# A cross-attention block on one core: values from a second copy of the context, their last rows as a pair, and one head scaled by VectorE

## What is computed

```
h = layernorm(x, gamma, beta)                       # x: 8 x 256 x 256
Q = h @ Wq;  K = context @ Wk;  V = context @ Wv    # context: 8 x 256 x 192; 1024 columns each
attn = softmax(Q K^T per head) * 64 ** -0.5
out = x + (attn V) @ Wo + bo
```

## Time and profile before

| | |
|---|---|
| median of 3 runs | 335.07 us (335.03 to 335.29) |
| the profiled execution | 335.13 us |
| its span, first to last instruction | 333.3 us |
| TensorE busy | 323.3 us, 97% |
| VectorE busy | 234.6 us, 70% |
| ScalarE busy | 254.8 us, 76% |
| GpSimd busy | 178.3 us, 53% |
| granted TensorE clock | 1.0, the 2.4 GHz level |

### The profile page before, as it was taken

How to read it: one execution, slowest core, us unless ns; L and a number is a source line. 1 busy time by engine, 2 the same in 40 slices (tenths; PEclk the granted TensorE clock), 3 DMA queues, 4 the chain that set the end, 5 groups by cost and what they waited for, 6 DMA issues and landing times.

```text
span 333.3 us, 9654 instructions
## 1 busy us (share of the span) xinstructions
PE 323.3 (97%) x3773; PEld 284.3 (85%) x3773; DVE 234.6 (70%) x523; ACT 254.8 (76%) x799; POOL 178.3 (53%) x332
## 2 busy tenths in 40 slices
PE   5999999999999999999999999999999999999986
PEld 4868788899888899888889988889988888998864
DVE  5888667766778677676776677776677867556754
ACT  4899897777778766888667868777777876676772
POOL 4596778437473367543673456722757336344430
PEclk9999999999999999999999999999999999999999
DMA  6960010020000200020000200002000100000000
GB/s 181 266 185 3 1 41 18 2 89 2 0 2 31 60 3 0 2 89 2 3 4 0 89 2 2 0 3 89 2 2 1 33 3 3 2 0 33 2 3 31
DMA packets 10764, 10.70 MB, mean 32 GB/s; under 512 B 960, under 2 KB 10176, under 8 KB 10720
## 3 DMA queue, kind: packets, MB, share of 16 engines
q1 hardware_dynamic: 10192, 9.64, 9.6%
q10 hardware_dynamic: 416, 0.33, 0.3%
q0 software_dynamic: 112, 0.13, 0.1%
HBM read 8.00 MB, written 2.10 MB: 30 GB/s over the span
## 4 chain that ended last, share of the span: by engine, by line
PE 86%; ACT 6%; DVE 4%; POOL 2%; DMA 1%; issue 1%; DVEq 0%; ACTq 0%
PE mix_ps L823 16%; PE o_ps L914 12%; PE ring_ps L794 12%; PE ring_ps L889 12%; PE ring_ps L968 11%; PE ring_ps L944 10%; PE ring_ps L847 9%; ACT prob L457 3%; DMA x_in<-in_x_dram 1%; PE ring_ps L867 1%; POOL prob L369 1%; PE mix_ps L760 1%; PE mix_ps L768 1%; ACT qk_hi L467 1%; DVE prob_t L737 1%
## 5 line engine op out<-in xcount | busy, mean ns | idle before, releaser
L369 POOL TENSOR_SCALAR prob<-prob,inv 128x256 f32<-128x256 f32 x256 | 120.4, 486 | 129.2 <-DVE inv L654 129.1
L457 ACT ACTIVATE prob<-ring_ps,neg_max 128x256 f32<-128x256 f32 x256 | 119.3, 481 | 21.7 <-DVE neg_max L647 21.6
L647 DVE TENSOR_REDUCE neg_max<-ring_ps 128x2 f32<-128x512 f32 x128 | 81.4, 679 | 0.8 <-PE ring_ps L794 0.8
L737 DVE COPY prob_t<-ring_ps 128x512 f32<-128x512 f32 x64 | 41.4, 686 | 37.0 <-PE ring_ps L944 37.0
L823 PE MATMUL mix_ps<-prob_t,v_sb 128*64 128x256 f32 x504 | 61.5, 385 | 0.2 <-DVE prob_t L737 0.2
L660 DVE TENSOR_TENSOR qk_lo<-ring_ps,qk_hi 128x512 fp32r<-128x512 f32 x64 | 44.2, 690 | 17.7 <-ACT qk_hi L467 17.7
L457 ACT ACTIVATION_READ_ACCUMULATOR prob<-ring_ps,neg_max 128x1 f32 x256 | 54.4, 212 | 0.0
L823 PEld LDWEIGHTS mix_ps<-prob_t,v_sb 128*64 128x64 f32 x504 | 33.4, 136 | 18.1 <-issue 0.3
L527 ACT ACTIVATE v_sb<-ring_ps 128x256 f32<-128x256 f32 x58 | 19.2, 383 | 30.1 <-PE ring_ps L968 29.6
L467 ACT ACTIVATE qk_hi<-ring_ps 128x512 fp32r<-128x512 f32 x64 | 39.6, 619 | 1.2 <-PE ring_ps L889 1.2
L944 PE MATMUL ring_ps<-ident,prob 64*128 64x64 f32 x1024 | 39.3, 226 | 0.3 <-POOL prob L369 0.3
(11 more groups left out here) (110 smaller groups left out, 638.2 us busy)
## 6 DMA issues: line engine op xcount, KB each, us to landing
x_in<-in_x_dram SPq DMA_DIRECT2D x8, 256.0 KB, 2.9
out_dram<-y_sb SPq DMA_DIRECT2D x7, 256.0 KB, 2.2
c_in<-in_ctx_dram SPq DMA_DIRECT2D x7, 192.0 KB, 2.8
w_raw<-in_L_xattn_Wq_dram SPq DMA_DIRECT2D x8, 128.0 KB, 3.1
w_raw<-in_L_xattn_Wo_dram SPq DMA_DIRECT2D x4, 256.0 KB, 4.0
w_raw<-in_L_xattn_Wk_dram SPq DMA_DIRECT2D x4, 128.0 KB, 3.7
w_raw<-in_L_xattn_Wk_dram SPq DMA_DIRECT2D x8, 64.0 KB, 3.5
w_raw<-in_L_xattn_Wv_dram SPq DMA_DIRECT2D x2, 256.0 KB, 4.7
```

Source lines behind the costliest of these rows:

```text
L369: last = nc.gpsimd.tensor_scalar(prob[:, e, r, :], prob[:, e, r, :], inv[:, e, r:r + 1], SCALE, ALU.mult, ALU.mult)
L457: last = nc.scalar.activation(prob[:, e, r, :], score_bank(u, e)[:, r * ROWS:(r + 1) * ROWS], ACT.Exp, bias=neg_max[:, e, r:r + 1], accum_ ...
L647: nc.vector.tensor_reduce(neg_max[:, e, :], score_bank(u, e)[:, :].rearrange("p (r j) -> p r j", r=RT), AX, ALU.max, negate=True).then_inc ...
L737: nc.vector.tensor_copy(turned_half(e), score_bank(u, e)[:, :] .rearrange("p (k i) -> p k i", i=HALF))\
```

## The change

It does five things.

- A second copy of the turned context, `c_val`, in a place of its own; GpSimd makes it with three copies per sequence (`context_for_values`), for the first sequence ahead of step 0, for the others at the end of the steps with u mod 4 = 0 (for the second in step 2). `values` reads its weights from `c_val` and waits for `c_val_ready`. The tiles behind move by 64 bytes (`wv_hi`, `wv_lo`) and by 6656 bytes (`v_sb` and all after it).
- From n = 3 on `values` makes four 128-row matmuls for each of its two banks and then, behind both, the last product as a pair of 64-row matmuls, one for each bank, from `c_rest` and the upper half of `c_val`.
- The fourth head is scaled by VectorE (`last_head`) instead of GpSimd; `turn` waits for three heads of GpSimd's and, in its second half, for VectorE's.
- From step 2 on (before: in step 2 alone) ScalarE copies `qk_hi` of the second pair ahead of the exp of head 3, and VectorE's `last_head` stands behind `qk_lo` of the second pair.
- The statistics of x are spread over their step instead of standing at its end, and those of the second sequence go to the end of step 0; its `x_norm` is made by GpSimd in step 1 instead of VectorE.

TensorE, in a step u with u mod 4 = 2: the two banks of `values` and the transposes `turn`, before, and then with the change.

The diff, without the declarations of semaphores; each piece begins with a line of "...":

```diff
...
         sb("shift4", [P, 4 * SHIFT])
         qk_lo = sb("qk_lo", [P, BATCH, 2, ROWS + SHIFT], fp32r)
-        sb("shift2", [P, 3 * SHIFT])
+        sb("shift2", [P, 4 * SHIFT])
         wv_hi = sb("wv_hi", [P, O0 - V0, INNER], fp32r)
         wv_lo = sb("wv_lo", [P, O0 - V0, INNER], fp32r)
         sb("shift3", [P, SHIFT])
+        c_val = sb("c_val", [P, 2, CT, ROWS], fp32r)
+        sb("shift5", [P, 7 * SHIFT])
         v_sb = sb("v_sb", [P, 2, RT, GROUP * P])
...
                 last.then_inc(x_norm_ready, 1)
 
+            def context_for_values(b):
+
+                if b >= 2:
+                    pool.wait_ge(v_made, PER_SEQ * (b - 1))
+                pool.wait_ge(c_lo_ready, b + 1)
+                for k in range(CT):
+                    last = nc.gpsimd.tensor_copy(c_val[:, b % 2, k, :], c_t[:, b % 2, k, :])
+                last.then_inc(c_val_ready, 1)
+
             def bias(b):
...
                 weight_lo(n)
             pool.dma_start(bo_b[:, :], b_o.partition_broadcast(P)).then_inc(bo_in, 16)
+            context_for_values(0)
 
...
                 if b is not None:
                     deviation(b)
-                    if b >= 2:
-                        norm(b)
+                    norm(b)
                 if u == PER_SEQ:
                     weight_lo(23)
                 if 0 <= u < STEPS:
-                    for e in range(HEADS):
+
+                    for e in range(HEADS - 1):
                         pool.wait_ge(inv_ready, HEADS * u + e + 1)
                         for r in range(RT):
                             last = nc.gpsimd.tensor_scalar(prob[:, e, r, :], prob[:, e, r, :],
                                                            inv[:, e, r:r + 1], SCALE,
                                                            ALU.mult, ALU.mult)
-                        last.then_inc(scaled, 1)
+                        last.then_inc(scaled_pool, 1)
                         if e == 1 and u == 2:
...
                 if b is not None:
                     hidden_lo(b)
+                b = 1 if u == 2 else of_seq(u, TURN_C, 2)
+                if b is not None:
+                    context_for_values(b)
+                b = of_seq(u, SPLIT_H, 1)
                 if u == 2:
...
                     weight_hi(20)
                     weight_hi(21)
+                if u >= 2:
                     keys_hi(1)
                 probabilities(3)
-                if u != 2:
+                if u < 2:
                     keys_hi(1)
...
                     .then_inc(w_lo_ready, 1)
 
-            def statistics(b):
+            def rows_statistics(b, r):
                 k = b % 2
                 dve.wait_ge(x_loaded[k], 16 * (b // 2 + 1))
-                for r in range(RT):
-                    last = nc.vector.bn_stats(bn[:, r, :], x_in[:, k, r, :])
-                last.then_inc(stats_done, 1)
-                dve.wait_ge(stats_done, b + 1)
+                nc.vector.bn_stats(bn[:, r, :], x_in[:, k, r, :]).then_inc(stats_done, 1)
+
+            def variance(b):
+                dve.wait_ge(stats_done, RT * (b + 1))
                 nc.vector.memset(var_eps[:, :], 0.0)
                 for r in range(RT):
                     last = nc.vector.bn_aggr(mean_var[:, r, :], bn[:, r, :])
                 last.then_inc(aggr_done, 1)
+
+            def deviation_base(b):
                 dve.wait_ge(aggr_done, b + 1)
                 nc.vector.tensor_scalar(var_eps[:, :], mean_var[:, :, 1], EPS, None, ALU.add)\
                     .then_inc(var_ready, 1)
+
+            def statistics(b):
+                for r in range(RT):
+                    rows_statistics(b, r)
+                variance(b)
+                deviation_base(b)
 
...
                         nc.vector.reciprocal(inv[:, e, :], sums[:, e, :]).then_inc(inv_ready, 1)
 
+                def last_head():
+
+                    inverse(HEADS - 1)
+                    if 0 <= u < STEPS:
+                        dve.wait_ge(inv_ready, HEADS * u + HEADS)
+                        for r in range(RT):
+                            last = nc.vector.tensor_scalar(prob[:, HEADS - 1, r, :],
+                                                           prob[:, HEADS - 1, r, :],
+                                                           inv[:, HEADS - 1, r:r + 1], SCALE,
+                                                           ALU.mult, ALU.mult)
+                        last.then_inc(scaled_vector, 1)
+
                 def keys_lo(a):
...
                 maximum(3)
                 inverse(1)
+
+                measured = of_seq(u, STATS, 2)
+                if measured is not None:
+                    rows_statistics(measured, 0)
                 b = of_seq(u, PUT)
...
                 if u == -1:
                     weight_lo(4)
+                if measured is not None:
+                    rows_statistics(measured, 1)
                 keys_lo(0)
+                if measured is not None:
+                    variance(measured)
                 if u == -1:
                     weight_lo(5)
-                if u != 2:
-                    inverse(3)
+                if u < 2:
+                    last_head()
                 b = of_seq(u, SPLIT_H, 1)
                 if b is not None:
...
-                if u == 0:
-                    statistics(1)
-                if u == 1:
-                    norm(1)
                 if u == 2:
                     weight_lo(20)
                     weight_lo(21)
                 keys_lo(1)
-                if u == 2:
-                    inverse(3)
+                if measured is not None:
+                    deviation_base(measured)
+                if u >= 2:
+                    last_head()
                 b = of_seq(u, TURN_C, 2)
                 if b is not None:
                     context_lo(b, context_bank(b))
-                b = of_seq(u, STATS, 2)
-                if b is not None:
-                    statistics(b)
                 if 0 <= u < STEPS:
...
                             .then_inc(prob_t_ready[1], 1)
                     if u == 0:
+                        statistics(1)
                         weight_lo(13)
...
 
                 for a in range(BATCH):
-                    pe.wait_ge(scaled, HEADS * u + 2 * a + 2)
+                    pe.wait_ge(scaled_pool, (HEADS - 1) * u + 2 + a)
+                    if a == BATCH - 1:
+                        pe.wait_ge(scaled_vector, u + 1)
                     for k, (h, j, r) in enumerate(itertools.product(range(2), range(RT), range(RT))):
...
 
 
+
                 g, j = divmod(n, RT)
                 b, half = divmod(g, 2)
                 rows = slice(j * P, (j + 1) * P)
                 if j == 0 and g in FOR_V:
                     high_ready(pe, FOR_V[g])
+                pe.wait_ge(c_val_ready, b + 1)
                 passes = context_products(wv_hi, wv_lo)
                 first = half * PIECE
-                for a, ps in enumerate(((mix_ps, o_ps, mix_ps)[n],) if n <= RT else qk_banks(n)):
-                    columns = PIECE if n <= RT else V_HALF
-                    if n > RT:
-
-                        pe.wait_ge(qk_lo_ready, BATCH * n + a + 1)
+                if n <= RT:
                     for m, (w, i, k) in enumerate(passes):
+                        if m == CT and j == 0:
+                            low_ready(pe, FOR_V[g])
+                        last = nc.tensor.matmul((mix_ps, o_ps, mix_ps)[n][:, :], c_val[:, b % 2, k, rows],
+                                                w[:, i, first:first + PIECE],
+                                                start=m == 0, stop=m == len(passes) - 1,
+                                                skip_group_check=True)
+                    last.then_inc(v_made, 1)
+                    return
+                for a, ps in enumerate(qk_banks(n)):
+
+                    pe.wait_ge(qk_lo_ready, BATCH * n + a + 1)
+                    for m, (w, i, k) in enumerate(passes[:-1]):
                         if m == CT and j == 0 and g in FOR_V:
                             low_ready(pe, FOR_V[g])
-                        last = nc.tensor.matmul(ps[:, 0:columns], c_t[:, b % 2, k, rows],
-                                                w[:, i, first:first + columns],
-                                                start=m == 0, stop=m == len(passes) - 1,
-                                                skip_group_check=True)
-                    first += columns
+                        nc.tensor.matmul(ps[:, 0:V_HALF], c_val[:, b % 2, k, rows],
+                                         w[:, i, first + a * V_HALF:first + (a + 1) * V_HALF],
+                                         start=m == 0, stop=False, skip_group_check=True)
+                pe.wait_ge(c_rest_ready, b + 1)
+                high = (c_rest[:, b % 2, rows], c_val[HALF:P, b % 2, 1, rows])
+                for a, ps in enumerate(qk_banks(n)):
+                    own = slice(a * HALF, (a + 1) * HALF)
```

(3 more changed lines are left out.)

4 lines of the change are left out of this document (3 added, 1 removed).

## The result

The changed kernel takes 338.93 us (median of 6 runs, 337.62 to 339.72), the kernel before 335.30 us beside it (6 runs, 335.03 to 335.54). The ratio of the means is 1.0104, with a 95% interval of 1.0078 to 1.0129: slower by 1%, where 332.7 us was forecast and 335.0 us was the upper end of the range. The profiled execution has 339.38 us and a span of 337.3 us, 4.0 us more than the kernel before; what lies outside the span is 2.1 us, where the kernel before had 1.8.

The account below looks back on a forecast made before the run. TensorE, busy 97% of the span, was taken to bound the kernel. 335.1 - 3.4 (pair) - 1.3 (second-bank wait) + 1.8 (VectorE/GpSimd collision) + 0.5 (start) = 332.7 us; range 330.2 to 335.0, 84%.

Parts of the forecast that it names:

- The statistics spread over gaps of VectorE in steps 3 mod 4: VectorE in steps 3 mod 4: moving the statistics of x into its idle gaps costs nothing.
- The slot of the pair: `values` on TensorE: two fifth matmuls become one half-height pair costing one slot; 29 groups x 0.118 us = 3.4 us saved.
- only moves ahead of the pair: TensorE ahead of `turn`: the existing cost of switching from 128 to 64 rows changes place, with no cost added.
- the sign that I gave: `values` group on TensorE, if the forecast is right: 0.12 us shorter in steps with transposes, 0.20 in the others.
- The second bank: `values` in 16 steps without transposes: ScalarE's earlier `qk_hi` removes TensorE's 0.08 us wait for `qk_lo`, 1.3 us saved.
- The new home of the weights: `values` reading `c_val`: matmul pace might move from 0.118 towards 0.113 us, at best 1.2 us gained; taken as none.
- The collision: Steps 6, 10, ... 26: VectorE's fourth-head scalings meet GpSimd's `h_lo` and `x_bias`; TensorE waits 0.3 us each, 1.8 us lost.
- The fourth head's price, rows 6 and 7: `turn`'s second half: VectorE's scalings end with 0.3 us of slack, costing nothing where VectorE runs undisturbed.
- The start: Steps 0 and 1: moved statistics and GpSimd's `x_norm`, against one head fewer for GpSimd, lose 0.5 us; bounds 0 to 1.9.
- `x_norm` got between no scalings: Rival, steps 3, 7, ... 23: VectorE's second scaling waits for one GpSimd `x_norm`, 6.6 us lost, 339.3 us; chance 10%.
- The pair didn't take two slots: Rival, `values`: the half-height pair takes two slots, so its 3.4 us gain is lost, 336.1 us; chance 6%.

## Why the prediction was wrong

**The step that failed** is one sentence, a term put at nothing: "The statistics spread over gaps of VectorE in steps 3 mod 4: nothing." It costs nothing in five of the six steps that it touches; in step 3 it puts an instruction that waits for a load in front of `mix_lo`, and costs 4.2 us in the profiled execution, 3.5 us by the medians of the kernel without it, and 4.3 us alone on the kernel before. I asked of that edit only whether VectorE had the time, not what the instruction waits for. The trace of the kernel before had the answer: `mix_lo` started at 47.13 us, ahead of the load's issue at 47.65. In later sequences the load is issued two steps ahead (that of x(3) at 73.03 us of the changed kernel, its statistics at 91.31); sequence 2 is the first that reuses a buffer. No rival covered it, and nothing in the list of what would show it. None of them had the clock either, which is over a third of the price, 1.6 us of 4.2.

**The slot of the pair**, 3.4 us: right in kind, and 2.0 us in size. The members do start 0.01 us apart, as the earlier trace rows had it. The failed part is "only moves ahead of the pair": the longer gap ahead of 64-row work is there ahead of the pair and again between the pair and the transposes. So the sign that I gave, a `values` shorter by 0.12 us with transposes and 0.20 without, did not come: it was 0.03 and 0.12, and `turn`, of which the sum had nothing, gave 0.06.

**The second bank**, 1.3 us: the wait is gone, in the 16 steps and by the reorder that was named. As a term it was sized alone, 0.08 us a step against the demand of the kernel before; against the earlier demand of the new one the same reorder is worth 0.22 us in 14 of the 16 steps, 3.5 us by the medians. The sum of the two terms isn't hurt by that, since the pair's term took its slot in these steps too; but it hides that without the reorder the pair gains nothing there. For steps 4 to 30 the two terms give 27 x 0.118 + 15 x 0.08 = 4.4 us, and the trace 3.5 (1.28 net, with the collision's 2.24 taken out), the better pace included.

**The new home of the weights**: "I take none". It is worth 1.0 us, near the bound of 1.2 that stood beside it. The 0.005 us a matmul that this bound was made of was right; to take nothing of it was the miss.

**The collision**, 1.8 us: right in steps and mechanism, and near in size, 6 x 0.373 = 2.2 us by the trace and 2.6 us with the kernel that avoids it. As drawn, the first scaling ends 0.15 us behind the second `h_lo`, and the second scaling behind one `x_bias`.

The Trainium skill, "SBUF — State Buffer", section "Who interferes with whom", says that a VectorE `tensor_scalar` in a two-port mode, and a `tensor_tensor` with both inputs in SBUF against a GpSimd operation that reads SBUF, wait for the shared pair of ports for a whole instruction. The trace agrees for both (0.35 us against 0.595 and 0.819 for the scalings; 1.28 against 1.82 for the two `wv_lo`), and I weighed it for the first only: the second is the 0.5 us of step 2, which no term of the sum had. It does not agree for GpSimd's `rstd`: in the steps 7, 11, .. 23 it takes 0.71 to 0.72 us on two numbers a row and starts some 0.26 us ahead of VectorE's first scaling, which takes its usual 0.35 us.

**The fourth head's price, rows 6 and 7**: "costs nothing in a step in which VectorE runs undisturbed" holds; from step 3 on `turn` waits for it in no step but those six.

**The start**, 0.5 us lost, bounded by 1.9: it lost 1.04 us in the profiled execution, of which 0.5 in step 1, where `x_norm` stands ahead of the heads on GpSimd as worked out, and 0.5 in step 2 by `wv_lo` beside `h_lo`; the rest, 0.3 us lost ahead of step 0 and 0.2 won in it, nearly cancels.

**The rivals.** `x_norm` got between no scalings: they take 0.35 us each in steps 3 mod 4 also. In step 7 `x_norm` starts at 96.12 us and the second scaling, begun at 95.76, ends at 96.11. The pair didn't take two slots. Both that were to make it slower were wrong, and it was slower by a third way.

Put together for the profiled execution, by stretches: up to step 3 the sum had 0.4 us lost (0.5 less the slot of step 2) and it was 1.04, which is 0.7 more; step 3 had 0.2 us to win (a slot and a wait) and lost 4.2, 4.4 more; steps 4 to 30 had 4.4 - 1.8 = 2.6 us to win and won 1.3, 1.3 less; 0.3 us lie behind step 31's start and outside the span. 332.7 + 0.7 + 4.4 + 1.3 + 0.3 = 339.4 us; 339.38 were measured. The other misses matter as well: without the loss of step 3 the kernel takes 335.40 us, 2.7 above the forecast, 0.4 above its range, and no faster than the kernel before.

## What to carry to other kernels

When an instruction is moved forward in a queue, ask first what it waits for, at the first use of every buffer and not in the steady state: its own time may fit a gap while its wait holds up all that stands behind it. Gains that lie in a row on one engine are worth what the latest input allows; here pair and second copy are worth 2.0 and 1.0 us, taken out one at a time, with ScalarE's new order, and 0.2 us together without it, so an edit should be priced with the others in place. An engine that is given less to do starts its next work earlier, and that work can fall beside another engine's: twice here (`x_bias`, `h_lo`) freeing GpSimd made VectorE slower.

## What the runs showed of the hardware

- The same matmuls with weights read from another place in SBUF start 0.113 us apart instead of 0.117 to 0.119; over 29 groups of eight and their pairs this was 1.0 us. What about the place makes the difference isn't shown.
- After 2.8 us nearly without work, TensorE was granted 0.50 of its clock for 2.7 us. It did not do so in every run: three of six had a mean granted clock of 1.0. The kernel with the spread statistics alone had 2.4 us without any matmul and then 0.51 for 2.7 us, and all four of its runs had a mean of 0.995.
- Between two 64-row matmuls that load together (0.01 us apart) and the transposes behind them lie 0.22 us, as much as between a 128-row matmul and either of them; 128-row matmuls in a row start 0.113 us apart.
- A GpSimd operation of 0.72 us on two numbers a row (`rstd`) beside VectorE's scalings lengthened neither of the two (353 and 350 ns); operations on whole tiles did lengthen VectorE's, copies (a cast 0.48 us for 0.27) as well as subtractions.
- The other way round, a VectorE operation on two numbers a row took 0.75 us beside GpSimd's subtraction of a tile and 0.17 behind it.
